# Issuing the first score matmul of a pair three times in five of the 32 score steps of each batch

## The reference

```python
scores = jnp.einsum('bhqd,bhkd->bhqk', q, k) * scale
scores = scores.at[:, :, 0, -1].set(NEG)
scores = scores.at[:, :, -1, 0].set(NEG)
weights = jax.nn.softmax(scores, axis=-1)
out = jnp.einsum('bhqk,bhkd->bhqd', weights, v)
```

## Time and profile before

| what | value |
|---|---|
| median of three executions | 1176.37 us |
| the profiled execution | 1178.01 us, span 1176.2 us |
| PE busy | 1047.0 us |
| VectorE (DVE) busy | 758.5 us |
| ScalarE (ACT) busy | 638.0 us |
| mean granted TensorE clock | 0.927 of full |

### The profile page before, as it was taken

How to read it: one execution, slowest core, us unless ns; L and a number is a source line. 1 busy time by engine, 2 the same in 40 slices (tenths; PEclk the granted TensorE clock), 3 DMA queues, 4 the chain that set the end, 5 groups by cost and what they waited for, 6 DMA issues and landing times.

```text
span 1176.2 us, 16225 instructions
## 1 busy us (share of the span) xinstructions
PE 1047.0 (89%) x5310; PEld 608.8 (52%) x5310; DVE 758.5 (64%) x1575; ACT 638.0 (54%) x860; POOL 149.2 (13%) x174
## 2 busy tenths in 40 slices
PE   5779989668998899899998999899989997998977
PEld 4434433335555465456555646465646554655754
DVE  3445645367658776877677857776778667625662
ACT  2335765334434748565765567566746574665522
POOL 2000000001200120022002200211021102111221
PEclk9789998878969999989997999799979999998988
DMA  4586675721041105110411141113211130030001
GB/s 129 133 224 200 184 217 165 228 78 28 23 158 46 28 8 166 53 33 15 162 49 33 27 152 46 45 27 106 92 45 27 41 140 19 1 126 19 1 1 36
DMA packets 91287, 97.39 MB, mean 83 GB/s; under 512 B 10547, under 2 KB 76790, under 8 KB 89174
## 3 DMA queue, kind: packets, MB, share of 16 engines
q1 hardware_dynamic: 91222, 96.63, 27.7%
HBM read 41.34 MB, written 29.36 MB: 60 GB/s over the span
## 4 chain that ended last, share of the span: by engine, by line
PE 65%; DVE 11%; ACT 8%; issue 6%; SPq 5%; DMA 4%; POOL 0%; DVEq 0%; ACTq 0%
PE y_ps L716 21%; PE x_ps L716 15%; PE st_ps L716 9%; PE pv_ps L716 7%; PE sm_ps L716 6%; PE y_ps L863 3%; ACT probs L1144 2%; ACT L1144 2%; DVE mx L1346 2%; SPq L572 2%; DMA a_scr<-a_cat 2%; PE y_ps L830 2%; DVE xn L1386 1%; ACT h_t L1144 1%; DVE xt_lo L1580 1%
## 5 line engine op out<-in xcount | busy, mean ns | idle before, releaser
L1346 DVE TENSOR_REDUCE mx<-sm_ps 128x2 f32<-128x1024 f32 x256 | 312.8, 1222 | 150.5 <-PE sm_ps L716 141.0
L1144 ACT ACTIVATE probs<-st_ps 128x1024 f32<-128x1024 f32 x256 | 262.2, 1024 | 176.0 <-PE st_ps L716 173.5
L716 PE MATMUL st_ps<-q_st,k_st 52*128 52x512 f32 x512 | 209.0, 472 | 14.6 <-ACT probs L1144 12.9
L716 PE MATMUL sm_ps<-k_st,q_st 50*128 50x512 f32 x512 | 176.5, 481 | 35.5 <-DVE mx L1346 21.2
L716 PEld LDWEIGHTS st_ps<-q_st,k_st 52*128 52x128 f32 x512 | 85.5, 193 | 121.0 <-issue 64.0
L716 PE MATMUL pv_ps<-probs,v_all 128*32 128x512 f32 x1024 | 146.0, 644 | 0.0
L716 PE MATMUL x_ps<-b_cat,pt 128*128 128x256 f32 x448 | 110.3, 384 | 0.0
L716 PEld LDWEIGHTS sm_ps<-k_st,q_st 50*128 50x128 f32 x512 | 67.6, 193 | 60.9 <-DVE mx L1346 31.8
L1144 ACT ACT_TABLE_LOAD x74 | 94.9, 1283 | 1.8 <-PEq L1830 0.7
L716 PEld LDWEIGHTS x_ps<-b_cat,pt 128*128 128x128 f32 x448 | 80.0, 190 | 18.7 <-issue 8.3
L475 POOL TENSOR_TENSOR px<-px,cst 128x512 f32<-128x512 f32 x56 | 57.9, 1044 | 227.9 <-DVE cst L1441 227.9
(11 more groups left out here) (299 smaller groups left out, 1760.1 us busy)
## 6 DMA issues: line engine op xcount, KB each, us to landing
a_scr<-a_cat SPq DMA_DIRECT2D x32, 512.0 KB, 5.4
a_cat<-a_scr SPq DMA_DIRECT2D x8, 2048.0 KB, 7.8
q_st<-qk_hi SPq DMA_DIRECT2D x128, 64.0 KB, 2.3
k_st<-qk_hi SPq DMA_DIRECT2D x128, 64.0 KB, 2.3
b_scr<-b_cat SPq DMA_DIRECT2D x8, 1024.0 KB, 8.5
b_cat<-b_scr SPq DMA_DIRECT2D x8, 1024.0 KB, 9.7
xa<-in_x SPq DMA_DIRECT2D x9, 512.0 KB, 3.7
q_st<-qk_lo SPq DMA_DIRECT2D x64, 64.0 KB, 2.3
```

The lines of the kernel that those rows point to most:

```text
L716: return nc.tensor.matmul(dst, lhs, rhs, start=start, stop=stop, **kw)
L1144: return nc.scalar.activation(dst, src, f, **kw)
L1346: nc.vector.tensor_reduce(mx[:, c % 2, :].rearrange("p (m x) -> p m x", m=2)[:, :, col], sm_ps[:], axis=AX, op=ALU.max).then_inc(sm_taken, 1)
```

## The change

In ticks 16, 18, 20, 22 and 24 of every iteration (chunk 1, key tiles 0, 1 and the first pair of 2) the first score matmul of the pair is issued three times instead of once, with the same operands into the same bank of `st_ps`, before anything else of the pair. Each starts its bank anew, so the bank holds the same in the end. No wait and no semaphore count changes. All later lines shift by one, and those after the loop by two.

```diff
+AGAIN = {16: 3, 18: 3, 20: 3, 22: 3, 24: 3}
...
-                last = mm(st_ps[:, r % 2], k_st[rows_, h, P * i:P * i + P], q_st[rows_, h, :], True, True)
+                for _ in range(AGAIN.get(e - r % 2, 1) if r % 2 == 0 else 1):
+                    last = mm(st_ps[:, r % 2], k_st[rows_, h, P * i:P * i + P], q_st[rows_, h, :], True, True)
                 if r % 2 == 1:
                     last.then_inc(st_full, 1)
```

## The result

Over 20 executions each, the changed kernel takes 1182.26 us (median; 1172.72 to 1195.42) and the kernel before 1176.04 us (1172.21 to 1178.69). The ratio is 1.0047, with a 95% interval of 1.0028 to 1.0066, so the change makes the kernel slower by about 5.5 us (3.3 to 7.8). All ratios here leave out executions over 1.5% above the fastest of their kernel, which are 1191.11 and 1195.42 us of the change, 1193.12 us of the second experiment and a lone 3150.86 us of the filled pause; with its own two kept in, the mean of the change lies 7.1 us above that of before. The spread is part of the result: that of before is 6.5 us, that of the change 22.7 us. The profiled execution took 1186.37 us, its span is 1184.5 us, which is 8.3 us longer than the span of before. Executions with a higher mean clock are the shorter ones: 1172.72 us came with 0.945, 1177.46 with 0.938, 1188.70 with 0.925.

What follows compares the result with a forecast made beforehand. PE was taken to bound the kernel, with 65% of the chain. Iterations 0 (2.3), 1 (0.5) and 3 to 6 (2.0) add 4.8 us, the clock gives back 2.3: 2.5 more, 1178.9 us against the median; range 1170.5 to 1185.

Steps and rivals of the forecast that it cites:

- the second rival: Nothing given back, iterations 2 and 3 become like 4 to 6: 7.7 us more, 1181 to 1184; chance 0.35.
- the third rival: Repeats cost and give nothing: within 1 us of 1176.4; chance 0.38 together with the forecast.
- first fall: Drop to half clock behind PE's 2.55 us stand ahead of WO, 743.0 to 749.9 in iteration 5.
- the first rival: Repeats hold the clock up, from tick 18 ahead of WO: 5 to 11 us less, 1165 to 1171; chance 0.27.
- The direction and the bound: PE holds 65% of the chain; added matmuls cost time where the rest waits for PE; forecast 2.5 us more.
- Ticks 16 and 18 hide: Two repeats fit PE's waits of 0.77 us (tick 16) and 0.95 us (tick 18) and cost nothing.
- The price of a repeat: Repeats on the same rows follow one another at full price: two cost 0.47 us at full clock, 0.86 at half.
- Iteration 0: 2.3 us: PE is bound by the setup there, so all ten repeats count at full clock: 2.3 us; lower bound nothing.
- the two signs by which the prediction called itself wrong: WO running at 0.12 us in most iterations, or iteration 0 not being longer.
- Iterations 3 to 6: 0.5 us each, from tick 22 at half clock, and nothing for tick 24: Tick 22's repeats delay X2 and S, tick 24's wait behind ScalarE's evacuations: 2.0 us more in all.
- What the clock gives: One of six iterations is spared the first fall, so WO runs at full clock there: 2.3 us less.
- second fall: Later drop to half clock, from tick 20's scores on, 753.3 to 760.1 in iteration 5.

Runs made afterwards that it cites:

- the second experiment: The change with its repeats only in ticks 20, 22 and 24, against the kernel before: ratio 1.0062, 7.3 us more.
- the filled pause: Kernel before, without repeats, plus eight all-row matmuls just ahead of WO in tick 18 of iterations 1 to 6: ratio 0.9955, 5.3 us less.
- the eleventh experiment: The change with its repeats only in iterations 2 to 7, against the kernel before: ratio 1.0024, median 1176.03 us, executions in two heaps.

## Why the prediction was right, and where it wasn't

The measured 1182.26 us lies in the range (1170.5 to 1185.0), but above the forecast of 1178.9, at the place of the second rival: slower, with little given back. I had given it 0.35 and the forecast and the third rival 0.38 together. The direction follows from the working; the size is in part luck, since three of the terms that make it up came out otherwise, as told below. Two slips in the working changed little: one first fall is worth 2.2 us by its own price (24 x 0.09) and was taken at 2.3, and the range starts at 1170.5, though the first rival was put at 1165 to 1171 and so lies almost all below it.

**The direction and the bound.** Right. PE holds more of the chain than before (69% against 65%), and the kernel is slower though the mean clock of its executions isn't lower.

**Ticks 16 and 18 hide.** Right as to the waits: in the profile after, iteration 5, the `for_max` matmul of tick 18 starts 0.95 us behind the pair's first score matmul (741.16 and 742.11), as before. Whether they are free in total is open: alone they measured 2.2 us, with an interval that starts at 0.1.

**The price of a repeat.** Right at full clock. In iteration 0, tick 18, PE starts the pair at 130.74 and the next work at 131.88, 1.14 us; before it was 130.45 to 131.11, 0.66 us. Two repeats are 0.48 us and the sum had 0.47.

**Iteration 0: 2.3 us.** Wrong at the place where it was to arise. The exponential of tick 26 moves from 143.2 to 144.5 us, 1.3 us and not 2.3, so not all ten repeats count. The iteration as a whole is 1.1 us shorter than before, which is one of the two signs by which the prediction called itself wrong. One profile each can't settle it, though: without any repeat in it this iteration took from 108.8 to 111.9 us in five profiles, with added matmuls from 109.1 to 112.7 in nine, the change's 109.8 among them. Repeats in iterations 0 and 1 alone measured 1.0004, with an interval up to 3.1 us. Between nothing and 2.8 us the term stays open, and I had taken nearly the upper end.

**Iterations 3 to 6: 0.5 us each, from tick 22 at half clock, and nothing for tick 24.** This is the step that failed. That repeats in half clock put X2 and S off was right. But I priced them inside half-clock stretches whose length I held fixed at 6.8 us, and the stretches became longer. One drawn-out stretch of 13.7 or 17.1 us costs 3 to 5 us (iteration 4: 126.1 against 123.1; iteration 5: 126.9 against 122.9; in the second experiment 128.1 against 123.1), and in the profile two of the four loop iterations had one. Tick 24 isn't free then: from its pair to the first H matmul PE takes 3.86 us (760.87 to 764.73), and before 2.29 (758.60 to 760.89), and ScalarE waits for PE behind it.

**What the clock gives.** I had counted one first fall fewer, 2.3 us. Four of the six iterations show a shorter first fall or one fall less: iterations 3 and 6 have only one, of 3.4 us, and 4 and 5 have 3.4 in place of 6.8. Iterations 2 and 7 have more half-clock time than before, as told above. In iterations 3 and 6, without a long second fall, the gain came to 0.1 and 0.7 us. So falls moved, as the second rival says, though not as it has it: iteration 3 got better, not like 4 to 6. The first rival, repeats hold the clock up, doesn't hold for this change: WO ran at 0.12 us throughout in none of the four loop iterations, and the kernel isn't faster. What does hold the clock up through WO is work inside the pause, which the filled pause showed (1.8 us from tick 16 to 18 in iterations 4 to 6, and 5.3 us in all).

**Two rules.** The Trainium skill ("TensorE: Matmul & The Clock Gate", Part 3: Packing small matmuls) says that matmuls on different groups of rows run at the same time, and that a weight load overlaps a running matmul only where their groups differ. The trace agrees: two matmuls on different halves start 0.01 us apart, and two repeats on the same half take 0.48 us. The Trainium skill also says that activity releases the slow clock (same page, Part 1, What's actually happening). That holds only in part here: over 17.10 us PE was busy by its record without a break and the clock stayed at 0.50, and with the same count and columns on all rows it came back after at most 6.8 us in these ticks.

**What stays open.** Why some executions have long stretches and others none: the same code took from 1172.72 to 1195.42 us. That the phase of an iteration against the clock's own decisions is behind it fits the two heaps of the eleventh experiment, but no run set that phase. Nor is it shown how the cost of 2 to 5 us divides that remains where no long stretch is seen (ticks 16 and 18, tick 20, all rows), or how much of the change's own loss is time on PE and how much is the long stretches.

## What to carry to other kernels

Added matmuls that are to keep TensorE's clock up are to be put inside the pause in which it stands: eight on all rows in each of six pauses, into a bank that was free, gave 5 us, while 80 repeats next to work that ran anyway took 5.5. (Half-row matmuls in the pause weren't tried.) A stretch at half clock isn't a fixed cost to which added work adds its doubled price; it can be longer afterwards, so look at what it lasts in the new profile. A higher mean clock isn't yet a gain: compare times. And where the clock falls, take many executions: one profile of a kernel whose times spread over 20 us can show either case.

## What the runs showed of the hardware

PE at 0.50 for 17.1 us while its record shows it busy for all of it is what I hadn't expected; in the kernel before the longest such stretch in these ticks was 6.8 us. Elsewhere the kernel before has it too, for 10.20 us of 10.20 in iteration 1 (336.9 to 347.1), so neither repeats nor half-row scores in ticks 16 to 24 are needed for it; only the length of 17.1 us is new.

A `for_max` matmul on the other half of the rows starts ahead of repeats that stand before it in PE's list, so that the lists run in order holds for tasks that wait, and not for the starts of such neighbours. In iteration 0 of the profile after, PE in order of time (in program order the three score matmuls of the even head come first, then `for_max`, then the second score matmul and `for_max`):

```profile
130.74 0.50 PE L717 MATMUL st_ps<-q_st,k_st 52*128 52x512 f32 x1
130.75 0.50 PE L717 MATMUL sm_ps<-k_st,q_st 50*128 50x512 f32 x1
131.08 0.63 PE L717 MATMUL st_ps<-q_st,k_st 52*128 52x512 f32 x3
131.56 0.39 PE L717 MATMUL sm_ps<-k_st,q_st 50*128 50x512 f32 x1
131.88 1.98 PE L717 MATMUL y_ps<-xn,pt 128*128 128x512 f32 x4
```

The first repeat starts 0.34 us behind the first score matmul, the `for_max` matmul 0.01 us behind it.
